# The second attention's slot table made by products of one-hot rows on the chip, and routing weights stored with the rows

## What is computed

```
x = x + attention0(norm(x), ctx)          # 16 heads, masked by layer index
x = x + experts0(norm(x))                 # top 2 of 8, no capacity
x = x + attention1(norm(x), ctx)          # both directions, gated by sigmoid
x = x + experts1(norm(x))                 # top 2 of 8, capacity 640 a expert
```

```
gate_logits = xt @ Wg + bg
top_v, top_i = top_k(gate_logits, 2)
seq = cumsum(one_hot(top_i).sum(1), axis=0) * one_hot(top_i).sum(1)
valid = (seq > 0) & (seq <= capacity)            # capacity = 640
flat_idx = where(valid, expert * capacity + seq - 1, none)
disp = rows of xt placed at flat_idx             # 8 experts x 640 slots
h = silu(disp @ W1) * (disp @ W2);  out = h @ W3
y = sum over the 2 picks of softmax(top_v) * out[slot of the pick]
```

## Time and profile before

| | |
|---|---|
| median of 3 runs | 1442.37 us (1441.47 to 1446.17) |
| profiled execution | 1439.13 us, of it 1437.4 us span |
| busy, share of the span | TensorE 93%, VectorE 60%, ScalarE 57%, GpSimd 47% |

### The profile page before, as it was taken

One profiled execution on the slowest core, in us unless ns is written; L12 is line 12 of the kernel. 1 busy time (PEld: TensorE's weight loads), 2 busy tenths in 40 slices (PEclk: granted clock), 3 DMA queues, 4 the chain that ended last, 5 costly groups with the idle time before them and its releaser, 6 DMA issues.

```text
span 1437.4 us, 37467 instructions
## 1 busy us (share of the span) xinstructions
PE 1340.9 (93%) x12922; PEld 1100.8 (77%) x12922; DVE 864.0 (60%) x2358; ACT 817.6 (57%) x1911; POOL 669.6 (47%) x939
## 2 busy tenths in 40 slices
PE   6999999998699999999996999999984999999996
PEld 5787778776556666666665899999973999999996
DVE  4778888888633323333331677778864666666664
ACT  4787877876255555555552555555543555555542
POOL 4235555555543333333322467777755344444322
PEclk9999999999799999999998999999996999999999
DMA  4345443432189999999994233333323444343431
GB/s 146 96 114 133 115 105 107 126 93 61 33 165 178 201 181 180 179 179 175 175 179 107 81 89 93 89 89 90 89 64 78 127 126 126 125 123 109 125 110 53
DMA packets 280921, 172.98 MB, mean 120 GB/s; under 512 B 213054, under 2 KB 259360, under 8 KB 280740
## 3 DMA queue, kind: packets, MB, share of 16 engines
q1 hardware_dynamic: 259156, 135.85, 41.3%
q0 software_dynamic: 18608, 32.21, 8.2%
q10 hardware_dynamic: 2976, 2.52, 0.7%
HBM read 93.44 MB, written 31.97 MB: 87 GB/s over the span
## 4 chain that ended last, share of the span: by engine, by line
PE 79%; DVE 6%; DMA 5%; issue 4%; ACT 3%; POOL 3%; ACTq 0%; SPq 0%; DVEq 0%; POOLq 0%
PE psum L2375 15%; PE psum L1473 12%; PE psum L1493 12%; PE psum L2391 7%; PE psum L1975 3%; PE psum L1894 3%; PE psum L1900 3%; PE psum L899 2%; PE psum L828 2%; PE psum L802 2%; PE psum L916 2%; PE psum L902 2%; DVE mx L1049 2%; PE psum L880 2%; PE psum L1965 2%
## 5 line engine op out<-in xcount | busy, mean ns | idle before, releaser
L2375 PE MATMUL psum<-d_xT,d_w 128*128 128x256 f16 (+1 forms) x2304 | 227.6, 255 | 0.0
L2375 PEld LDWEIGHTS psum<-d_xT,d_w 128*128 128x128 f16 x2304 | 199.0, 98 | 18.9
L1393 DVE SCALAR_TENSOR_TENSOR b_h<-b_hid,b_h 128x1024 f16<-128x1024 f32 x71 | 87.0, 1225 | 202.2 <-ACT b_h L1428 202.2
L1473 PE MATMUL psum<-arena,b_xT 128*128 x852 | 196.9, 381 | 10.1 <-DMA b_xT<-b_x 9.0
L1493 PE MATMUL psum<-arena,b_hT 128*128 x1704 | 197.7, 273 | 2.3 <-DMA b_hT<-b_h 2.2
L1493 PEld LDWEIGHTS psum<-arena,b_hT 128*128 128x128 f16 x1704 | 166.2, 98 | 37.6 <-issue 4.4
L1303 POOL DMA_INDIRECT b_xg<-dram_normed,b_gi x71 | 69.2, 975 | 200.4 <-issue 145.1
L1473 PEld LDWEIGHTS psum<-arena,b_xT 128*128 128x128 f16 x852 | 83.7, 98 | 98.9 <-issue 14.9
L2435 ACT ACTIVATE d_sg<-psum 128x256 f32<-128x256 f32 (+1 forms) x192 | 66.6, 347 | 139.2 <-PE psum L2375 139.2
L2493 DVE SCALAR_TENSOR_TENSOR d_hf<-psum,d_sg 128x256 f32<-128x256 f32 (+1 forms) x192 | 72.1, 379 | 99.1 <-ACT d_sg L2435 95.4
L1421 ACT ACTIVATE b_hid<-psum 128x512 f32<-128x512 f32 x142 | 83.5, 596 | 59.1 <-PE psum L1473 57.4
(11 more groups left out here) (320 smaller groups left out, 2979.8 us busy)
## 6 DMA issues: line engine op xcount, KB each, us to landing
d_wst<-in_L_w SPq DMA_DIRECT2D x64, 384.0 KB
stage<-in_L_w SPq DMA_DIRECT2D x32, 512.0 KB, 3.7
dram_expert_rows<-b_ys SPq DMA_DIRECT2D x71, 128.0 KB
ctxT<-in_ctxT SPq DMA_DIRECT2D x64, 128.0 KB, 2.1
dram_normed<-xn SPq DMA_DIRECT2D x64, 128.0 KB, 3.2
x<-in_x SPq DMA_DIRECT2D x32, 128.0 KB, 4.1
dram_x<-xnew SPq DMA_DIRECT2D x32, 128.0 KB, 3.1
c_x<-dram_x SPq DMA_DIRECT2D x32, 128.0 KB, 3.2
```

Of the source, the lines that this page charges most:

```text
L1393: dve.scalar_tensor_tensor(out=h16[:, p, 1, :], in0=hid[:, p, :], scalar=H_SCALE, in1=h16[:, p, 0, :], op0=ALU.mult, op1=ALU.subtract).the ...
L1473: i = pe.matmul(psum[:, 1 + 2 * p + half, :], xT[:, j % NT, px, c, :], weights(e, c, pw, half * 512, 512), start=(n == 0), stop=(n == len( ...
L2375: i = pe.matmul(psum[:, q, m * n:(m + 1) * n], w16[:, fc % RING, pw, col:col + P], xT[:, p, px, c, at:at + n], start=(k == 0), stop=(k == ...
```

## The change

The table `ids1`, its fill, its 64 scatters and its read-back are gone. In their place:

- **Slots split** (`split`, VectorE, end of turn c + 3): the slot number is cut in its low seven bits (which partition of a 128-slot chunk) and the rest (which of 40 chunks).
- **One-hot rows** (`one_hots`, VectorE): for each block and pick two rows per token, 128 wide for the partition and 40 wide for the chunk, the second multiplied by a code of the token number. They stand at the very end of a turn, behind the residual: blocks 0, 1, 2, 3 of a group in turns 7, 8, 8, 9 after the group's first block; at the end, blocks 24 and 25 in turn 31, 26 to 29 in turn 32, 30 in turn 33, 31 in turn 34.
- **Table products** (`table`, TensorE, ahead of the logits): the product of both one-hots, summed over tokens, is a 128 x 40 table of codes. Six tables of four blocks (8 products each), one of six blocks, one of two.
- **Adding and decoding** (`add_table`, `decode`, VectorE): the tables are summed in SBUF, and the codes turned to token numbers at once in `gi`, where GpSimd's gathers read them.
- **Dense weights** (`dense`, VectorE): the weights of a token for all 8 experts, stored by SP behind the token's row: rows of `xs[1]` have now 264 columns, and the gathers bring the weight with the row. The second experts copy the expert's column out of the gathered row before each low half.
- SP loads the third and fourth weight unit of the second experts at the end of the second attention; GpSimd waits for the stored rows and weights and for the decoded table, gathers the rows of expert 0, and only then waits for the output rows. A later gather waits for the low half of the tile that it overwrites, no longer for its transposes.
- GpSimd makes two more constant tables while the first experts run.

```diff
-        xs = [dram(f"normed{l}", (T + 1, D)) for l in range(2)]
+        xs = [dram(f"normed{l}", (T + 1, D + l * E)) for l in range(2)]
-        ids = [dram_ids("ids0", SPARE0 + P, 2), dram_ids("ids1", SPARE1, 2)]
+        ids = [dram_ids("ids0", SPARE0 + P, 2)]
...
+            def made_in(b):
+                if b < NB - 2 * RG:
+                    return b // RG * RG + (7, 8, 8, 9)[b % RG]
+                return (NB - 1, NB - 1, NB, NB, NB, NB, NB + 1, NB + 2)[b - NB + 2 * RG]
+            TABLES = [(b, RG) for b in range(0, NB - 2 * RG, RG)] + [(NB - 2 * RG, RG + 2), (NB - 2, 2)]
+            def table_in(t):
+                return RG * t + 11 if t < 6 else NB + 1
...
             def c_sync(sp, first_weights, next_weights):
...
+                def store_w(g):
+                    first, n = GROUPS[g]
+                    sp.wait_ge(dense_ready, g + 1)
+                    sp.dma_start(xs[1][first * P:(first + n) * P, D:D + E].rearrange("(j p) e -> p j e", p=P), gwd[:, g % 2, 0:n, :]
+                                 ).then_inc(wd_st[g % 2], 16)
...
                     store_n(b - 2)
                     store(b - 1)
+                    if last_of(b - 4) is not None:
+                        store_w(last_of(b - 4))
...
             def c_pool(pool):
-                def scatter(b, k):
...
-                    pool.indirect_dma_start(ids[1], bass.IndirectOffsetOnAxis(ap=gsidx[:, g % NS, at:at + 1], axis=0),
-                                            gsidw[:, g % NS, at, :], None, bounds_check=bound, oob_is_err=False).then_inc(scat[g % NS], 16)
...
             def c_pe(pe):
...
+                def table(t):
+                    first, n = TABLES[t]
+                    pe.wait_ge(hot1_ready, first + n)
+                    for m in range(n):
+                        for k in range(2):
+                            j = place(first + m)
+                            i = pe.matmul(psum[:, 7, TAB:TAB + E * CBLK], hotp[:, j, k, :], hott[:, j, k, :], start=(m == 0 and k == 0),
+                                          stop=(m == n - 1 and k == 1))
+                    i.then_inc(tab_done, 1)
...
             def c_dve(dve, slot_tokens, ids_ready):
...
+                def dense(g):
+                    n = GROUPS[g][1]
+                    dve.wait_ge(w_ready, g + 1)
...
+                    dve.tensor_tensor(gwx[:, 0:2 * n, :], ghot[:, 0:2 * n, :], cols(gw2[:, 0:2 * n], E), ALU.mult).then_inc(dense_steps, 1)
+                    dve.wait_ge(dense_steps, g + 1)
...
+                    dve.tensor_tensor(gwd[:, g % 2, 0:n, :], two[:, :, 0, :], two[:, :, 1, :], ALU.add).then_inc(dense_ready, 1)
+                def split(g):
+                    q, n = g % 3, GROUPS[g][1]
+                    dve.wait_ge(slot_ready, g + 1)
+                    dve.tensor_scalar(prow_i[:, q, 0, 0:2 * n], gsidx[:, q, 0:2 * n], P - 1, None, ALU.bitwise_and)
+                    dve.tensor_scalar(prow_i[:, q, 1, 0:2 * n], gsidx[:, q, 0:2 * n], 7, None, ALU.logical_shift_right).then_inc(split_steps, 1)
+                    dve.wait_ge(split_steps, g + 1)
+                    dve.tensor_copy(prow_f[:, q, :, 0:2 * n], prow_i[:, q, :, 0:2 * n]).then_inc(split_ready, 1)
+                def one_hots(b):
+                    g, j, n = group_of[b]
+                    q, at = g % 3, place(b)
+                    dve.wait_ge(split_ready, g + 1)
...
+                    for k in range(2):
+                        c = 2 * j + k
+                        dve.tensor_scalar(hotp[:, at, k, :], iota128[:, :], prow_f[:, q, 0, c:c + 1], None, ALU.is_equal)
+                        i = dve.tensor_scalar(hott[:, at, k, :], iota128[:, 0:E * CBLK], prow_f[:, q, 1, c:c + 1], code1[:, b:b + 1],
+                                              ALU.is_equal, ALU.mult)
+                    i.then_inc(hot1_ready, 1)
+                def add_table(t):
...
+                        dve.tensor_tensor(tabsum[:, :], new, tabsum[:, :], ALU.add).then_inc(tab_read, 1)
+                def decode(slot_tokens, ids_ready):
...
                 for b in range(NB + 3):
                     softmax(b)
                     g = last_of(b - 3)
                     if g is not None:
                         weights_out(g)
+                        if last_of(b - 2) is not None or b == NB + 2:
+                            dense(g)
...
                     residual(b - 1)
+                    for t in range(len(TABLES) - 1):
+                        if table_in(t) == b:
+                            add_table(t)
+                    if g is not None:
+                        if last_of(b - 2) is None and b < NB + 2:
+                            dense(g)
+                        split(g)
+                    for c in range(NB):
+                        if made_in(c) == b:
+                            one_hots(c)
+                add_table(len(TABLES) - 1)
+                decode(slot_tokens, ids_ready)
...
             def d_pool(pool):
...
+                for p in range(2):
+                    pool.wait_ge(xs_st[p], 16 * NB // 2)
+                    pool.wait_ge(wd_st[p], 16 * N_WD // 2)
+                pool.wait_ge(ids_ready, 1)
+                for k in range(CBLK):
+                    gather(0, k)
...
                 def low_x(e, p, k):
                     dve.wait_ge(xhi, CBLK * e + k + 1)
+                    at = e * CBLK + k
+                    dve.tensor_copy(wt[:, at:at + 1], xg[:, p, k, D + e:D + e + 1])
```

More of the change, by code:

```diff
@@ L1694, in c_sync @@
                     sp.wait_ge(xs_st[p], nth(NB - 2 + p))
-                for p in range(NS):
-                    sp.wait_ge(scat[p], scattered(len(GROUPS) - NS + (p - len(GROUPS)) % NS))
+                    sp.wait_ge(wd_st[p], nth(len(GROUPS) - 2 + p))
             def c_pool(pool):
-                bound = pool.to_reg(SPARE1 - 1)
                 def gather(b):
@@ L2012, in count @@
                         pe.wait_ge(cnt_read, g)
+                    if tables_made:
+                        pe.wait_ge(tab_read, len(tables_made))
                     cum, tot = E, E + RG * E
@@ L2288, in first_weights, with next_weights @@
                     load_weights(sp, u, u)
+            def next_weights(sp):
+                for u in range(2, 4):
+                    load_weights(sp, u, u)
             def d_sync(sp):
-                for i, (first, last) in enumerate(((0, CBLK), (CBLK, E * CBLK))):
-                    sp.dma_start(slot_ids[:, first:last, :], ids[1][first * P:last * P, :].rearrange("(j p) a -> p j a", p=P),
-                                 allow_slow_non_contiguous=True).then_inc(d_ids[i], 16)
                 def body(e, p):
@@ L2298, in body @@
                         load_weights(sp, e * FC + fc + 4, fc)
-                for u in range(2, 4):
-                    load_weights(sp, u, u)
                 for e in range(E):
@@ L2308, in d_pool @@
                 pool.wait_ge(d_clear, 1)
-                for i, (first, last) in enumerate(((0, CBLK), (CBLK, E * CBLK))):
-                    pool.wait_ge(d_ids[i], 16)
-                    pool.tensor_copy(gi[:, first:last], slot_ids[:, first:last, 0:1].rearrange("p k a -> p (k a)")).then_inc(d_idx, 1)
-                    pool.wait_ge(d_idx, i + 1)
-                    if i == 0:
-                        for k in range(CBLK):
-                            pool.indirect_dma_start(xg[:, 0, k, :], None, xs[1], bass.IndirectOffsetOnAxis(ap=gi[:, k:k + 1], axis=0)).then_inc(g_ld[0][k], 16)
                 def offsets(e, k):
@@ L2338, in store_rows @@
                                             bounds_check=last_row, oob_is_err=False).then_inc(row_st, 16)
+                for p in range(2):
[4 more added lines that the diff above has]
+                    gather(0, k)
+                for p in range(2):
+                    pool.wait_ge(x3_st[p], 16 * NB // 2)
                 for k in range(CBLK):
@@ L2507, in add_rows @@
                     if is_expert(e):
-                        for i in range(2):
-                            dve.wait_ge(d_ids[i], 16)
                         dve.wait_ge(row_ld, 16 * CBLK * (e + 1))
```

138 lines of the change are left out of this document (77 added, 61 removed).

## The result

The changed kernel takes **1450.8 us** (median of 20 executions, 1442.9 to 1454.9), the kernel before 1441.9 beside it (20, 1439.0 to 1449.0): ratio 1.0055, 95% interval 1.0041 to 1.0068. Forecast were 1451.0 and "slower"; the difference is small, 0.55%, but clear of 1.

A forecast was written before the change was run, and what follows sets the result against it. TensorE, just ahead of a nearly full VectorE, was taken to pace the second attention's loop. Terms +9.9 (loop), +1.1 (turn 30), -2.5 (tail), +0.1 (second experts) gave +8.6: 1442.37 to 1451.0 us, range 1439 to 1458.

The forecast's parts named there:

- Lateness passes one for one through ScalarE to TensorE: Second attention's loop: late VectorE softmax reductions delay TensorE; 37.36 us per four turns instead of 35.13, +9.9 over turns 6-29.
- The allowance of 0.65: Softmax reduction in the loop may come 0.65 us later than quiet before TensorE waits, in every type (turn number modulo 4).
- One-hots 0.72 a block: VectorE behind the residual: two 128-wide instructions at 0.20 us and two 40-wide at 0.16, 0.72 a block.
- The rival at 0.42: Cheap one-hots on VectorE, 0.42 us a block: +1.1 us in all, 1443.5; chance 0.11.
- Table products 0.29 a group: TensorE in the loop: eight small products per group of four blocks add 0.29 us in type 3, five times before turn 28.
- Late gathers, -2.1: Loop, turns 6 to 30: without scatters GpSimd's late gathers vanish, giving back 2.1 us.
- Turn 30, +1.1: Turn 30 of the second attention: 0.36 us of lateness plus 0.75 of slot splitting on the chain, +1.1.
- The tail, -2.5: From the last residual's statistics to the first expert gather: 13.5 us instead of 16.0, so -2.5.
- Second experts, +0.1: Second experts: 264-column rows and a weight column copied before each low half, +0.1 us; the rest under TensorE's products.
- Only the queue: Rival: lateness does not reach TensorE; VectorE's sum, 36.41 us per four turns, sets the loop: +3.9, 1446.2; chance 0.15.
- It fits: Rival: TensorE tolerates 1.5 us lateness and one-hots cost 0.42, so VectorE's work lies under TensorE's: 1437.6; chance 0.10.
- dear one-hots: Rival: one-hots on VectorE cost 1.0 us a block, 3.35 per four turns: +17.0 in all, 1459.4; chance 0.09.

The follow-up runs named there:

- e1: Changed kernel with VectorE's added work moved from behind the residual into the next turn's softmax wait for exponentials, until turn 31; ratio to the kernel before 0.9961.
- e3: Kernel before, scatters kept, plus four unused VectorE instructions of the one-hots' shapes per block behind the residual; ratio to the kernel before 1.0048.
- e10b: e8 with the one-hots of blocks 0 to 23 on GpSimd, one block a turn between its two norms; ratio to the kernel before 0.9959.
- e5: Changed kernel with the edits of e1 and e4 together; ratio to the kernel before 0.9967.
- e6: e5 with the one-hots of blocks 24 to 27 made by GpSimd in turns 31 and 32; ratio to the kernel before 0.9948.
- e8: e5 with the one-hots of blocks 28 and 29 made in turn 33 and the last two tables of four blocks each; ratio to the kernel before 0.9954.
- e7: e4 with the one-hots of blocks 0 to 27 made by GpSimd at the end of its turn; ratio to the kernel before 1.0148.
- e9b: e4 with the one-hots of blocks 0 to 23 on GpSimd, one block a turn between its two norms; ratio to the kernel before 0.9987.
- e4: Changed kernel with GpSimd's clearing of the row sums moved from behind its last norm to turn 1; ratio to the kernel before 1.0031.
- e2: Changed kernel with VectorE's added work ahead of the residual instead of behind it, until turn 30; ratio to the kernel before 0.9997.

## Why the prediction was right, step by step

- **Lateness passes one for one through ScalarE to TensorE.** Right, and it carries the forecast. Per four turns 37.29 against 37.36. Waits over the quiet periods: 0.24, 0.95, 0.02, 0.96 for types 0 to 3 (forecast 0.07, 0.69, 0.36, 0.82), at lateness 0.82, 1.54, 0.89, 1.53 (0.72, 1.34, 1.01, 1.47). Shown from both sides by e1 and e3.
- **The allowance of 0.65** was a little large: 1.54 - 0.95 = 0.59 and 0.82 - 0.24 = 0.58. In type 2 it is at least 0.87 (0.89 late, 0.02 lost), because the eight counting products stand between score and gate products there and push TensorE's own need back by their 0.29 (gate products 2.50 behind the score product and not 2.21). Taking one number, read in a turn of type 3, for all four types was the shortcut; the errors cancel.
- **One-hots 0.72 a block**: mis-sized, 0.82; the wide one right at 0.20, the narrow one 0.21 and not 0.16. An instruction 40 wide with two per-partition scalars costs as much as one 128 wide. The rival at 0.42, and with it the price of the Trainium skill ("VectorE: DVE Perf Modes", section on the TRN2 errata), an estimated 0.13 and 0.08, is refuted by the rows for this form.
- **Table products 0.29 a group**: mis-sized, nothing. From the end of the transposes of the probabilities to the mixing products (L1971) it is 1011.60 - 1010.95 = 0.65 with tables, 1001.92 - 1001.28 = 0.64 without. The tables fill a wait: the mixing products need ScalarE's copy of the probabilities, which is done at 1001.86 and 1011.53, and start 0.06 and 0.07 behind it both times:

```profile
1001.48 0.38 ACT L1830 ACTIVATE c_prT<-psum 128x256 f32<-128x256 f32 x1 [0.46 <-PE psum L1958]
...
1011.15 0.38 ACT L1830 ACTIVATE c_prT<-psum 128x256 f32<-128x256 f32 x1 [0.46 <-PE psum L1958]
```

  The timeline shows no gap there, as the modelled length of the logits covers nearly all of it. e10b, with all tables, has the length that the prediction gave for before without any wait.
- **Late gathers, -2.1**: right for the changed kernel, in which VectorE waited for gathered rows once in these turns (0.30 us; before nine times, 7.4 us), and 210.80 in e10b against 212.86 fits. But a GpSimd without scatters does not by itself end them: e1, e5, e6 and e8 have three or four such waits each, 1.25 to 2.7 us. The lighter GpSimd alone was not tried.
- **Turn 30, +1.1**: as a whole wrong, -0.6; the term itself nearly right, since with the clock taken out it is +0.9. I had not looked at the clock there. In the kernel before, block 31's gate products met a low one, the windows of both kernels over these products (us of TensorE's products, its weight loads, VectorE, ScalarE and GpSimd, then granted clock, DMA share and GB/s) being

```profile
1069.20:1072.80 3.60, 3.57 (x16) 3.27 (x16) 1.19 (x8) 0.60 (x1) 2.88 (x6) 0.53 0.71 210
```

```profile
1086.60:1088.70 2.10, 2.10 (x22) 2.04 (x21) 2.00 (x11) 0.60 (x1) 1.06 (x3) 1.00 0.68 132
```

  before 0.53, near the 1.2 GHz level; in the changed kernel 1.00, the 2.4 GHz level. 1.55 us of the miss of 1.7: 24.54 against 25.18 - 1.55 = 23.63 leaves +0.9 for the lateness and the splitting. Why the clock was low is not settled. Ahead of those products TensorE had waited 0.59, 0.20 and 0.59 us in the kernel before; in e3, which adds only VectorE's work, the same waits (0.59, 0.20, 0.58) stand ahead of the same products, and they took 2.02. e7 and e9b took 3.76 and 3.75, all others 2.02.
- **The tail, -2.5**: wrong, 0.0. Its pieces: 1.0 for the clearing, which before lay in GpSimd's wait for the scatters (the earlier trace rows begins after it) and is now beside the one-hots (e4: -0.97); 0.6 for six blocks at 0.82 instead of 0.72; 0.5 for the logits, late through `cnt_read`, which I had taken to follow the rows alone; 0.2 for GpSimd's start of the gather, 0.72 from the last index and not 0.51. Together 2.3 of 2.5.
- **Second experts, +0.1**: +0.3, within what that stage moves. The wider rows: from the first gather to the first product 7.19 against 7.11, with a landing of 3.47 in the changed kernel's chain against 2.76, for another gather of the row. Over all traces that stretch is 7.19 to 7.79 with the wider rows and 7.11 in both kernels without them (before and e3), but no run changes the rows alone. The estimate from the Trainium skill ("DMA: Bandwidth & Descriptors"), one or two tenths, is not contradicted and not shown.
- **Rivals.** "Only the queue" fails by the 0.59 that VectorE idles in a turn in which it is late, and is what e2 becomes. "It fits" fails; "dear one-hots" too. The whole, +8.9 between the medians against +8.6, owes its precision to cancelling: against the forecast +0.2 in the loop, -1.7 in turn 30, +2.5 in the tail, +0.3 behind it and -0.6 ahead of turn 6 (68.14 to 67.57), where I had put nothing; the median of before lay 0.5 lower than the one I started from.

## What to carry to other kernels

Ask of added work not only how much of an engine it takes, but which wait it stands in front of: 1.64 us behind a residual that itself waits for TensorE cost 0.95 in that turn, the same 1.64 in a wait for another engine cost it nothing. The second queue has the same rule (one norm behind 4.7 us of GpSimd's work made TensorE wait 3.1 us and cost 1.4 more in clock), so look there for a gap, not for a low busy share. And when an operation that lay in someone's wait loses its cover, look at what it now runs beside.

## What the runs showed of the hardware

- **GpSimd's clearing stops VectorE's one-hots.** 1.16 us of MEMSET, and two one-hots end with it, after 1.39 and 1.25 us instead of 0.30 and 0.28; with the clearing moved (e4) none of that tail takes more than 0.30. In e4 the same clearing (1.19 us) ran beside a reduction out of PSUM and small operations, which kept their 0.42 and 0.16. The Trainium skill ("SBUF — State Buffer", section "SBUF: two separate sides") states that VectorE in a two-port mode and GpSimd hold one pair of ports exclusively, the other blocking for a whole instruction. The trace agrees in the main (1.0 us lost of 1.16), though the first of the two one-hots had started 0.20 ahead of the clearing and still ended with it, and no run shows whether the one-hots are in such a mode. Weighed beforehand, the page would have pointed at that microsecond.
- **GpSimd's one-hots** take 0.60 to 0.63 us in the median of each run (128x128, float32 to float16) and 0.50 to 0.51 (128x40), single ones up to 0.88 and 0.78, against VectorE's 0.20 and 0.21 from start to start. Beside them VectorE's operation on 128x256 took up to 0.64 (e7; 0.59 in e10b) and not 0.48, its pair on 128x128 at worst 0.83 and not 0.49.
- **A wait of 2.0 us and more ahead of TensorE's transposes can cost a second time.** In five of six such turns of e7 the granted clock fell behind it (mean of the turn 0.86 or 0.87, 1.4 to 1.7 us more), in the sixth it stayed at 1.00; which of the two happens is not settled here.
